# Attention in a four-layer kernel: maxima added by unit matrix products, values split by ScalarE and VectorE, by-key logits ahead of the weighing

## The chip, the cores and the metric

One core of a Trainium2 chip runs the whole program in one launch. The metric is the device time of one execution, in microseconds (us): the kernel before takes 1793.18 us, the median of three runs (1792.56 to 1794.38). The engines are PE (TensorE, matrix products; PEld its weight loads), DVE (VectorE), ACT (ScalarE), POOL (GpSimd) and SP (SyncE, which here issues nearly all DMAs). PSUM has 8 banks per partition; PE writes only there, POOL reads and writes only SBUF.

## The reference

Four layers on x of shape 16 x 14 x 14 x 192, each with a group norm before it and a residual sum behind it: a GRU over the 196 positions, attention (l1), a mixture of 8 experts with 2 chosen per token, attention again (l3). The change is in the attention, 16 images, 196 tokens, 12 heads of 16 channels:

```python
q, k, v = (qkv[0], qkv[1], qkv[2])
rel_h = jnp.einsum('bhwc,hkc->bhwk', qr, Rh)
rel_w = jnp.einsum('bhwc,wkc->bhwk', qr, Rw)
bias = rel_h[..., :, None] + rel_w[..., None, :]
attn = jnp.einsum('bqd,bkd->bqk', q * scale, k)
attn = attn + bias.reshape(B * nh, N, N)
attn = jax.nn.softmax(attn, axis=-1)
out = jnp.einsum('bqk,bkd->bqd', attn, v)
```

Results are held close to float32: an operand is split into a high part rounded to fp32r and a low part (the rest), and products are summed over the parts.

## The kernel before

`attention_layer` is called twice, for l1 and l3, with the same loop. It first makes q and k (`item`), v (`value`) and the position terms (`rel`), and stores q, k and `rel` to DRAM. Then comes the main loop: IMAGES = 96 steps, one step for one image and one pair of heads (6 pairs x 16 images), with LAG = 4. Each engine runs its own list of work in program order; semaphores are the only order between them.

For image g of the loop the work is:

- `logits_by_query(g)` (PE, L1159): four products, queries in partitions and keys in columns, into two banks that exist once. Only the maxima are taken from them.
- VectorE (L1388): the maximum of each query over the keys, 98x784 to 98x4, in PSUM; then a cast to bf16 (L1393) and the rest in bf16 (L1395), into `mt`.
- `maxima_to_rows(g)` (PE, L1168): four products with a diagonal of ones turn `mt` into two rows; ScalarE copies these (L1316) into rows 0 and 1 of q, against which k holds rows of -1. So the next product subtracts the maximum.
- `logits_by_key(g)` (PE, L1180): four products, keys in partitions and queries in columns, with the maximum subtracted, into one of two pairs of banks. It waits for L1316 and for the exponentials of g - 2.
- ScalarE: the exponential twice, rounded (`ph`, L1325) and in float32 (`p32`, L1328). POOL: `pl` = `p32` - `ph` (L1080), in a ring of 3.
- `weigh_values(g)` (PE, L1197 and L1198): eight products of v (high and low part, and a column of ones) with `ph` and `pl`, into one bank. VectorE copies out the 64 product rows (L1361) and the 2 rows of sums (L1364); the next weighing waits for both copies.

v is split into its two parts by POOL (`split_values`, L1047 and L1051), for four images at a time in two head parts, spread over the three steps that follow each fourth step. Every eighth step VectorE takes a reciprocal of the sums (L1368).

In 28 of the 96 steps (1 to 7, 11 to 17, 33 to 39, 43 to 49, `rel_of_step`) a `rel` item of the next four heads runs as well: six products on PE (L1144 to L1146), a rounding on ScalarE (L1290), a subtraction on VectorE (L1353). Its bank exists once, so PE's next `rel` waits for VectorE's subtraction. Items 1 to 7 of 14 and 8 to 14 are of two shapes, with a DRAM store of the tile between them.

The order of a step i is written out by hand. On PE: `logits_by_query(i)`, `maxima_to_rows(i - 1)`, `rel`, `weigh_values(i - 4)`, `logits_by_key(i - 1)`. On VectorE: the maximum of i with cast and rest, the two copies of i - 4, `rel`, the reciprocal. On ScalarE: the copy of the maxima of i - 1, the exponentials of i - 2, `rel`. SP loads q, k, `rel` and, as a fourth piece, two zero rows of q for a quarter of the next pair, spread over the steps.

Of the kernel before, what the change touches and what calls it, by code (L numbers as in the profile page):

```python
# [7 lines left out]
ALU = mybir.AluOpType  # L8
# [702 lines left out]
ROWS = 106  # L711
Q_ROWS, REL_ROWS = 2, 50
# [33 lines left out]
def attention_layer(nc, tag, ins, x_in, y_out, qk_dram, rel_dram, sums_dram, rec_dram, given=None, kept=None, extra=(), taken=None, ahead=None, x_here=None, x_stored=None):  # L746
# [8 lines left out]
    LOADS, SLOTS, LOWS = 4, 3, 3  # L755
    PARTS = 4
    EACH = B // PARTS
    with Scope(nc, tag) as s:
# [43 lines left out]
        mt, ones_at = s.sb("mt", [128, 4, 2], bf16), s.sb("ones_at", [128, TH], bf16)  # L802
# [18 lines left out]
        s_summed, mx_ready, mh_ready, ml_ready = (s.sem(n) for n in "s_summed mx_ready mh_ready ml_ready".split())  # L821
        x_ready, x_copied, t_summed, p_high, p_ready, pl_ready = (s.sem(n) for n in "x_ready x_copied t_summed p_high p_ready pl_ready".split())
# [23 lines left out]
        def rel_sums(r):  # L846
            return ps[:56, rel_bank(r), :448].rearrange("p (u b w) -> p u b w", u=2, b=B)

# [17 lines left out]
        with nc.Block() as block:  # L866
            @block.sync
            def _(sp):
# [43 lines left out]
                def load(p, part, piece):  # L912
# [14 lines left out]
                    dst, row, src = ((q, Q_ROWS, qk[0]), (k, Q_ROWS, qk[1]), (q, REL_ROWS, rel), (q, 0, k[ROWS:ROWS + 2]))[piece]  # L927
                    rows = 2 if piece == 3 else src.shape[0]
# [26 lines left out]
                def main_step(i):  # L955
                    p, b = divmod(i, B)
                    part, piece = divmod(b - EACH - 1, LOADS)
                    if i < IMAGES and p + 1 < PAIRS and part >= 0:
                        load(p + 1, part, piece)
                    if i < IMAGES and p > 0 and part < 0:  # L960
                        load(p, (b + B - EACH - 1) // LOADS, (b + B - EACH - 1) % LOADS)
# [49 lines left out]
            def _(pool):  # L1011
# [24 lines left out]
                def split_values(n):  # L1036
                    p, part = divmod(n, 4)
                    halves, slots = slice(8 * part, 8 * part + 8), slice(n % 2 * 8, n % 2 * 8 + 8)
                    def whole(head):
                        return v[:TH, halves, 32 * p + HD * head:32 * p + HD * head + HD]  # L1040

                    def place(head, low):
                        at = 32 * head + HD * low
                        return vs[:TH, slots, head, at:at + HD]

                    def high(head):
                        pool.tensor_copy(place(head, 0), whole(head)).then_inc(vh_ready, 1)  # L1047

                    def low(head):
                        pool.wait_ge(vh_ready, 2 * n + head + 1)  # L1050
                        pool.tensor_tensor(place(head, 1), whole(head), place(head, 0).bitcast(f32), ALU.subtract).then_inc(vl_ready, 1)  # L1051

                    return high, low

# [15 lines left out]
                for n in range(2):  # L1070
                    high, low = split_values(n)
                    for head in range(2):
                        high(head)
                    for head in range(2):
                        low(head)
                for g in range(IMAGES):
# [5 lines left out]
                    if 5 <= g < IMAGES - 4 and g % 4:  # L1082
                        n = (g + 3) // 4
                        high, low = split_values(n)
                        if g % 4 == 1:
                            pool.wait_ge(o_summed, 4 * n - 4)
                            high(0)
                        if g % 4 == 2:
                            high(1)
                            low(0)  # L1090
                        if g % 4 == 3:
                            low(1)
# [11 lines left out]
            def _(pe):  # L1104
# [44 lines left out]
                def logits_by_query(g):  # L1149
# [3 lines left out]
                    if g >= 1:  # L1153
                        pe.wait_ge(ml_ready, g)
# [8 lines left out]
                def maxima_to_rows(g):  # L1163
                    pe.wait_ge(ml_ready, g + 1)
                    if g >= 1:
                        pe.wait_ge(x_copied, g)
                    for n in range(4):
                        last = pe.matmul(ps[64:66, R_BANK, n * TH:n * TH + TH], mt[:TH, n, :], ones_at[:TH, :], start=True, stop=True)  # L1168
                    last.then_inc(x_ready, 1)

                def logits_by_key(g):
                    b = g % B
                    pe.wait_ge(x_copied, g + 1)
                    if g >= 2:
                        pe.wait_ge(p_ready, g - 1)
                    queries = slice(b * T, (b + 1) * T)
                    for head in range(2):
                        for half in range(2):
                            keys = slice(b * T + half * TH, b * T + (half + 1) * TH)
                            last = pe.matmul(ps[:TH, T_BANK + 2 * (g % 2) + head, half * T:half * T + T], k[:, head, keys],  # L1180
                                             q[:, head, queries], start=True, stop=True)
                    last.then_inc(t_summed, 1)
# [1248 lines left out]
```

## Time and profile before

| what | value |
|---|---|
| median of 3 timed runs | 1793.18 us |
| profiled execution, first to last instruction | 1796.6 us |
| first maximum of l1's main loop starts at | 642.8 us |
| last copy of the sums of l1's main loop starts at | 905.45 us |
| last maximum of l3's main loop starts at | 1737.1 us |
| PE, VectorE, ScalarE, POOL busy over the span | 83%, 71%, 54%, 48% |

The profile is of one execution. Its span is from the first to the last instruction; what lies around it is not in the profile. A row of time says when an instruction (or a merged row of several, "x4") started, how long it took, and in brackets how long its engine had been idle before it and what ended that. PE's matrix products overlap: their spacing, not their length, is what each costs.

### The profile page before, as it was taken

The page shows a single profiled execution, that of the slowest core. Times are in us where ns is not written, and L with a number is a line of the kernel's source. Part 1 is how long each engine was busy: PE and PEld are TensorE (multiplying, and loading weights), DVE is VectorE, ACT ScalarE, POOL GpSimd, SP SyncE. Part 2 cuts the span into 40 slices and gives each one's busy share as a digit, 9 for nine tenths or more (in the row PEclk, how much of TensorE's full clock was granted, in tenths as well). Part 3 has the DMA queues.
Part 4 walks back from the last instruction along what each step waited for, and adds up shares of the span by engine and source line. Part 5 has one row for each costly group of instructions (what it writes and reads, how often), then busy time and mean ns, then how long its engine had stood idle before and what let it go on. Part 6 is the DMA issues. An engine that isn't in the chain of part 4 may idle for free. (4 is left out here: it accounts for less than half of the span.)

```text
span 1796.6 us, 51708 instructions
## 1 busy us (share of the span) xinstructions
PE 1485.9 (83%) x19315; PEld 1272.1 (71%) x19315; DVE 1269.7 (71%) x4444; ACT 973.4 (54%) x1990; POOL 855.0 (48%) x1080
## 2 busy tenths in 40 slices
PE   4868888888876888889977999899998697888978
PEld 4757777777765776767755667678774586777766
DVE  7877787877778567879956684544446646888974
ACT  3633333333344567889924234555543556888972
POOL 2712222222235056879952111456551416787984
PEclk9955555555558889999986589899995798999998
DMA  3000000000002596667215204322225468666712
GB/s 87 1 20 4 4 5 4 4 4 4 4 3 83 171 257 151 147 156 161 58 48 173 98 24 151 125 81 86 83 73 153 144 159 254 166 147 150 146 29 58
DMA packets 72178, 165.21 MB, mean 92 GB/s; under 512 B 17938, under 2 KB 43162, under 8 KB 69436
## 3 DMA queue, kind: packets, MB, share of 16 engines
q1 hardware_dynamic: 66556, 149.05, 31.3%
q0 software_dynamic: 5376, 12.85, 2.3%
q8 instruction: 158, 2.59, 0.6%
q14 instruction: 88, 0.72, 0.1%
HBM read 93.84 MB, written 67.42 MB: 90 GB/s over the span
## 5 line engine op out<-in xcount | busy, mean ns | idle before, releaser
L1080 POOL TENSOR_TENSOR l_arena<-l_arena,l_arena 98x784 fp32r<-98x784 f32 x192 | 358.4, 1872 | 91.3 <-ACT l_arena L1328 79.0
L514 PE MATMUL gru_ps_r<-gru_hp,gru_wp 128*128 128x16 f16 x3920 | 200.1, 176 | 68.1 <-DVE gru_hp L489 68.1
L514 PEld LDWEIGHTS gru_ps_r<-gru_hp,gru_wp 128*128 128x128 f16 x3920 | 150.8, 106 | 88.5 <-DVE gru_hp L489 88.5
L567 POOL TENSOR_TENSOR gru_kept<-gru_keep,l0s_state 128x32 f32<-128x32 f32 x196 | 49.3, 251 | 305.4 <-ACT gru_keep L582 305.4
L1388 DVE TENSOR_REDUCE l_ps<-l_ps 98x4 f32<-98x784 f32 x192 | 187.5, 977 | 9.1 <-PE l_ps L1159 3.2
L514 PE MATMUL gru_ps_n<-gru_hp,gru_wp 128*128 128x16 f16 x3920 | 191.1, 174 | 0.0
L1197 PE MATMUL l_ps<-l_arena,l_arena 128*66 128x196 f32 x768 | 162.1, 264 | 20.9 <-POOL l_arena L1080 20.1
L580 ACT ACTIVATE gru_reset<-gru_ps_r,gru_unscale 128x32 f32<-128x32 f32 x196 | 56.4, 288 | 216.8 <-PE gru_ps_r L514 216.8
L1325 ACT ACTIVATE l_arena<-l_ps 98x784 fp32r<-98x784 f32 x192 | 158.4, 825 | 4.6
L1328 ACT ACTIVATE l_arena<-l_ps 98x784 f32<-98x784 f32 x192 | 157.0, 818 | 0.0
L1198 PE MATMUL l_ps<-l_arena,l_arena 128*66 128x196 f32 x768 | 155.0, 255 | 0.0
L514 PEld LDWEIGHTS gru_ps_n<-gru_hp,gru_wp 128*128 128x128 f16 x3920 | 150.0, 104 | 0.0
L1197 PEld LDWEIGHTS l_ps<-l_arena,l_arena 128*66 128x66 f32 x768 | 106.5, 139 | 41.0 <-POOL l_arena L1080 30.8
L1316 ACT ACTIVATE l_arena<-l_ps 2x392 fp32r<-2x392 f32 x192 | 94.1, 490 | 74.0 <-PE l_ps L1168 67.3
L1159 PE MATMUL l_ps<-l_arena,l_arena 128*98 128x196 f32 x768 | 110.7, 267 | 18.8 <-DVE l_mt L1395 13.7
L1159 PEld LDWEIGHTS l_ps<-l_arena,l_arena 128*98 128x98 f32 x768 | 85.6, 168 | 34.3 <-DVE l_mt L1395 25.3
L1198 PEld LDWEIGHTS l_ps<-l_arena,l_arena 128*66 128x66 f32 x768 | 107.0, 139 | 1.2
L1361 DVE COPY l_arena<-l_ps 64x196 f32<-64x196 f32 x192 | 67.7, 353 | 54.5 <-PE l_ps L1198 51.0
L1180 PE MATMUL l_ps<-l_arena,l_arena 128*98 128x196 f32 x768 | 103.5, 258 | 0.0
L1144 PE MATMUL l_ps<-l_arena,l_arena 128*56 128x224 f32 x168 | 59.8, 356 | 43.1 <-DVE l_arena L1353 40.4
L2231 DVE TENSOR_TENSOR l_arena<-mx_ps,l_arena 128x512 fp32r<-128x512 f32 x56 | 38.7, 692 | 77.9 <-ACT l_arena L2039 52.2
L1838 POOL DMA_INDIRECT picked<-l_arena,mx_target x56 | 55.3, 987 | 71.9 <-DVE l_arena L2238 60.5
(389 smaller groups left out, 4568.9 us busy)
## 6 DMA issues: line engine op xcount, KB each, us to landing
l_arena<-qk SPq DMA_DIRECT2D x96, 294.0 KB
qk<-l_arena SPq DMA_DIRECT2D x48, 392.0 KB, 9.0
rel<-l_arena SPq DMA_DIRECT2D x24, 686.0 KB
l_arena<-rel SPq DMA_DIRECT2D x48, 343.0 KB
qk<-l_arena SPq DMA_DIRECT2D x12, 784.0 KB, 7.9
l_arena<-in_experts_dram SPq DMA_DIRECT2D x8, 1152.0 KB, 7.6
l_arena<-x SPq DMA_DIRECT2D x24, 294.0 KB, 5.3
l_arena<-x SPq DMA_DIRECT2D x24, 196.0 KB, 3.1
```

The costliest lines, as they stand in the source:

```text
L514: last = pe.matmul(out[:, b, B * m:B * m + B], wp[:, wi, g, m, :], hp[:, b, part, B * k:B * k + B], start=False, stop=True, skip_group_che ...
L1080: pool.tensor_tensor(pl[g % LOWS][:TH, :, :], p32[:TH, g % 2, :, :], ph[:TH, g % 4, :, :].bitcast(f32), ALU.subtract).then_inc(pl_ready, 1)
L1144: pe.matmul(out, rh[:, n, :], line(high), start=True, stop=False)
L1159: last = pe.matmul(ps[:TH, S_BANK + head, half * T:half * T + T], q[:, head, queries], k[:, head, keys], start=True, stop=True)
L1180: last = pe.matmul(ps[:TH, T_BANK + 2 * (g % 2) + head, half * T:half * T + T], k[:, head, keys], q[:, head, queries], start=True, stop=True)
L1197: pe.matmul(out, values, ph[:, g % 4, head, cols], start=head == 0 and keys == 0, stop=False)
L1198: last = pe.matmul(out, values, pl[g % LOWS][:, head, cols], start=False, stop=head == 1 and keys == 1)
L1316: act.activation(q[0:2, :, b * T:(b + 1) * T], ps[64:66, R_BANK, :TB].rearrange("p (h t) -> p h t", h=2), ACT.Copy).then_inc(x_copied, 1)
L1325: act.activation(ph[:TH, g % 4, :, :], banks, ACT.Exp).then_inc(p_high, 1)
L1328: act.activation(p32[:TH, g % 2, :, :], banks, ACT.Exp).then_inc(p_ready, 1)
L1361: dve.tensor_copy(o_quad[p // 2][row:row + 64, b * T:(b + 1) * T], ps[:64, O_BANK, :T]).then_inc(o_kept, 1)
L1388: dve.tensor_reduce(m, ps[:TH, S_BANK:S_BANK + 2, :TB].rearrange("p c (h k) -> p c h k", h=2), AXIS.X, ALU.max).then_inc(mx_ready, 1)
```

## The change

- The maxima no longer go through rows of q. VectorE writes the negated maximum straight into `mt` (fp32r, in SBUF, a ring of 2). After the four by-key products, still in the same accumulation, PE adds four products: a column of `mt` broadcast to 98 columns as weights, and a unit matrix, read twice, as the moved operand of 196 columns. So each by-key logit gets the negative maximum of its query. `maxima_to_rows`, the cast, the rest and ScalarE's copy go; q and k lose two rows (ROWS 106 to 104), and SP's fourth load piece goes.
- On PE `logits_by_key(i - 1)` with the unit products now comes ahead of `weigh_values(i - 4)`, behind `rel`.
- v is split by ScalarE (`round_values`, behind the exponentials in two of four steps) and VectorE (`lower_values`, between the maximum and the copies in two of four steps), not by POOL. The first two parts are made ahead of the loop.

```diff
-    LOADS, SLOTS, LOWS = 4, 3, 3
+    LOADS, SLOTS, LOWS = 3, 3, 3
-        mt, ones_at = s.sb("mt", [128, 4, 2], bf16), s.sb("ones_at", [128, TH], bf16)
+        mt, unit = s.sb("mt", [128, 2, 4], f32r), s.sb("unit", [128, TH], f32r)
...
                 def logits_by_key(g):
                     b = g % B
-                    pe.wait_ge(x_copied, g + 1)
                     if g >= 2:
                         pe.wait_ge(p_ready, g - 1)
+                    both = unit[:TH, :].rearrange("p (a t) -> p a t", a=1).to_broadcast([TH, 2, TH])
                     for head in range(2):
+                        bank = ps[:TH, T_BANK + 2 * (g % 2) + head, :TB]
                         for half in range(2):
-                            last = pe.matmul(ps[:TH, T_BANK + 2 * (g % 2) + head, half * T:half * T + T], k[:, head, keys],
-                                             q[:, head, queries], start=True, stop=True)
+                            pe.matmul(bank[:, half * T:half * T + T], k[:, head, keys], q[:, head, queries],
+                                      start=half == 0, stop=False, skip_group_check=True)
+                    pe.wait_ge(max_ready, g + 1)
+                    for head in range(2):
+                        bank = ps[:TH, T_BANK + 2 * (g % 2) + head, :TB].rearrange("p (k t) -> p k t", k=2)
+                        for half in range(2):
+                            n = 2 * head + half
+                            last = pe.matmul(bank[:, :, half * TH:(half + 1) * TH], mt[:TH, g % 2, n:n + 1].to_broadcast([TH, TH]), both,
+                                             start=False, stop=half == 1, skip_group_check=True)
                     last.then_inc(t_summed, 1)
...
                     if i < IMAGES:
                         logits_by_query(i)
-                    if 1 <= i <= IMAGES:
-                        maxima_to_rows(i - 1)
                     if i in rel_of_step:
                         rel(rel_of_step[i])
+                    if 1 <= i <= IMAGES:
+                        logits_by_key(i - 1)
                     if i >= LAG:
                         weigh_values(i - LAG)
-                    if 1 <= i <= IMAGES:
-                        logits_by_key(i - 1)
...
+                def round_values(n, head):
+                    act.activation(value_parts(n, head, 0), values_of(n, head), ACT.Copy).then_inc(vh_ready, 1)
...
-                        act.activation(q[0:2, :, b * T:(b + 1) * T], ps[64:66, R_BANK, :TB].rearrange("p (h t) -> p h t", h=2), ACT.Copy).then_inc(x_copied, 1)
...
                         act.activation(p32[:TH, g % 2, :, :], banks, ACT.Exp).then_inc(p_ready, 1)
+                        n = g // 4 + 1
+                        if g >= 6 and n < IMAGES // 4 and g % 4 in (2, 3):
+                            act.wait_ge(o_summed, 4 * n - 4)
+                            round_values(n, g % 4 - 2)
...
+                def lower_values(n, head):
+                    dve.wait_ge(vh_ready, 2 * n + head + 1)
+                    dve.tensor_tensor(value_parts(n, head, 1), values_of(n, head), value_parts(n, head, 0).bitcast(f32), ALU.subtract).then_inc(vl_ready, 1)
...
                 for i in range(IMAGES + LAG):
                     if i < IMAGES:
                         dve.wait_ge(s_summed, i + 1)
-                        m = ps[:TH, S_BANK, 400:404]
-                        dve.tensor_reduce(m, ps[:TH, S_BANK:S_BANK + 2, :TB].rearrange("p c (h k) -> p c h k", h=2),
-                                          AXIS.X, ALU.max).then_inc(mx_ready, 1)
-                        dve.wait_ge(mx_ready, i + 1)
-                        if i >= 1:
-                            dve.wait_ge(x_ready, i)
-                        dve.tensor_copy(mt[:TH, :, 0], m).then_inc(mh_ready, 1)
-                        dve.wait_ge(mh_ready, i + 1)
-                        dve.tensor_tensor(mt[:TH, :, 1], m, mt[:TH, :, 0], ALU.subtract).then_inc(ml_ready, 1)
+                        if i >= 2:
+                            dve.wait_ge(t_summed, i - 1)
+                        dve.tensor_reduce(mt[:TH, i % 2, :], ps[:TH, S_BANK:S_BANK + 2, :TB].rearrange("p c (h k) -> p c h k", h=2),
+                                          AXIS.X, ALU.max, negate=True).then_inc(max_ready, 1)
+                    n = i // 4
+                    if 8 <= i < IMAGES and i % 4 in (2, 3):
+                        lower_values(n, i % 4 - 2)
                     if i >= LAG:
                         keep_products(i - LAG)
```

## Rows read from the trace of the kernel before

**Rows 1.** The page's first line.

```profile
span 1796.6 us, 51708 instructions
```

**Rows 2.** Windows of the maxima, L1388: stretch, its length, busy time, count, clock.

```profile
802.30:893.50 91.20, 40.29 (x41) 1.00 0.57 121
```

**Rows 3.** Windows, plain steps: PE, PEld, VectorE, ScalarE, POOL busy (count), clock, DMA.

```profile
802.30:893.50 91.20, 83.87 (x821) 69.91 (x820) 83.23 (x211) 83.19 (x124) 90.32 (x95) 1.00 0.57 121
```

**Rows 4.** Lines by group, same stretch: count, busy us, mean ns, idle before.

```profile
L1080 POOL TENSOR_TENSOR l_arena<-l_arena,l_arena 98x784 fp32r<-98x784 f32 x42 | 78.5, 1873 | 1.9 <-ACT l_arena L1328 1.5
...
L1368 DVE RECIPROCAL l_sums<-l_sums 98x32 f32<-98x32 f32 x5 | 1.6, 330 | 0.0
```

**Rows 5.** Timeline of VectorE in one plain step: start us, length us.

```profile
828.48 0.35 DVE L1361 COPY l_arena<-l_ps 64x196 f32<-64x196 f32 x1
...
829.26 0.98 DVE L1388 TENSOR_REDUCE l_ps<-l_ps 98x4 f32<-98x784 f32 x1
830.27 0.17 DVE L1393 CAST l_mt<-l_ps 98x4 bf16<-98x4 f32 x1
...
830.67 0.36 DVE L1361 COPY l_arena<-l_ps 64x196 f32<-64x196 f32 x1
```

**Rows 6.** Waits, 640 to 910 us: us in total, times, longest.

```profile
DVE l_arena L1361 <- PE l_ps L1198: 25.1, 34, 1.6
PEld l_ps L1144 <- DVE l_arena L1353: 21.9, 22, 3.4
```

**Rows 7.** Timeline of PE in a step with a `rel` item of the second shape.

```profile
783.98 0.39 PE L1144 MATMUL l_ps<-l_arena,l_arena 128*56 128x224 f32 x1 [0.78 <-DVE l_arena L1353]
...
785.22 0.28 PE L1197 MATMUL l_ps<-l_arena,l_arena 128*66 128x196 f32 x1
785.33 0.25 PE L1198 MATMUL l_ps<-l_arena,l_arena 128*66 128x196 f32 x1
...
785.97 0.53 PE L1180 MATMUL l_ps<-l_arena,l_arena 128*98 128x196 f32 x4
786.34 0.53 PE L1159 MATMUL l_ps<-l_arena,l_arena 128*98 128x196 f32 x4
...
787.91 0.39 PE L1144 MATMUL l_ps<-l_arena,l_arena 128*56 128x224 f32 x1 [0.78 <-DVE l_arena L1353]
```

**Rows 8.** Timeline of VectorE in the same step.

```profile
786.17 0.35 DVE L1361 COPY l_arena<-l_ps 64x196 f32<-64x196 f32 x1 [0.97 <-PE l_ps L1198]
...
786.94 0.92 DVE L1353 TENSOR_TENSOR l_arena<-l_ps,l_arena 56x448 fp32r<-56x448 f32 x1
```

**Rows 9.** Timeline of PE in a `rel` step of the first shape.

```profile
752.04 0.32 PE L1144 MATMUL l_ps<-l_arena,l_arena 128*56 128x224 f32 x1 [0.48 <-DVE l_arena L1353]
...
755.16 0.32 PE L1144 MATMUL l_ps<-l_arena,l_arena 128*56 128x224 f32 x1 [0.49 <-DVE l_arena L1353]
```

**Rows 10.** Timeline, other stages: the nearest sizes from SBUF to SBUF.

```profile
557.78 0.19 DVE L159 TENSOR_TENSOR l_arena<-l_arena 96x32 f32<-96x32 f32 x1
...
1059.96 0.53 ACT L2014 ACTIVATE l_arena<-l_arena 128x392 fp32r<-128x392 f32 x1 [0.62 <-DVE l_arena L2189]
```

**Rows 11.** Timeline of the experts layer: VectorE and POOL at once.

```profile
965.13 0.60 POOL L1515 TENSOR_TENSOR l_arena<-l_arena,l_arena 64x196 fp32r<-64x196 f32 x1 [0.28 <-ACT l_arena L1568]
965.19 0.77 DVE L1624 TENSOR_TENSOR l_arena<-l_arena,l_arena 128x196 fp32r<-128x196 f32 x1
```

**Rows 12.** Timeline ahead of l1: two POOL casts merged, and VectorE.

```profile
559.11 5.54 POOL L1019 CAST l_arena<-l_arena 128x3136 fp32r<-128x3136 f32 x2 [7.66 <-DMA l_arena<-in_attention_const_dram]
...
559.58 2.37 DVE L168 SCALAR_TENSOR_TENSOR l_arena<-l_arena 96x32 f32<-96x32 f32 x1
```

**Rows 13.** One line, L1624: least, median, greatest ns.

```profile
L1624 DVE TENSOR_TENSOR l_arena<-l_arena,l_arena x16: 346/350/772, 963.5 to 997.0; 128x196 fp32r<-128x196 f32 x16
```

**Rows 14.** Timeline of VectorE at the end of the loop of l1.

```profile
895.89 0.98 DVE L1388 TENSOR_REDUCE l_ps<-l_ps 98x4 f32<-98x784 f32 x1
...
905.45 0.36 DVE L1364 COPY l_arena<-l_ps 2x196 f32<-2x196 f32 x1
```

More of the change, by code:

```diff
@@ L710 @@
 QUADS = HEADS // 4
-ROWS = 106
-Q_ROWS, REL_ROWS = 2, 50
+ROWS = 104
+Q_ROWS, REL_ROWS = 0, 48
 AT_REL = 4 * N
@@ L847, in rel_sums, with values_of, value_parts @@
             return ps[:56, rel_bank(r), :448].rearrange("p (u b w) -> p u b w", u=2, b=B)
+        def values_of(n, head):
+            halves = slice(8 * (n % 4), 8 * (n % 4) + 8)
+            at = 2 * HD * (n // 4) + HD * head
+            return v[:TH, halves, at:at + HD]
+        def value_parts(n, head, low):
+            slots = slice(n % 2 * 8, n % 2 * 8 + 8)
+            at = 32 * head + HD * low
+            return vs[:TH, slots, head, at:at + HD]
         rel_of_step = {2 * B * quad + at: REL * (quad + 1) + j for quad in range(QUADS - 1) for j, at in enumerate(REL_STEPS)}
@@ L926, in load @@
                     rel = rel_dram[quad].rearrange("(g h r) c n -> g r c h n", g=2, h=2)[at].rearrange("r c h n -> (r c) h n")
-                    dst, row, src = ((q, Q_ROWS, qk[0]), (k, Q_ROWS, qk[1]), (q, REL_ROWS, rel), (q, 0, k[ROWS:ROWS + 2]))[piece]
-                    rows = 2 if piece == 3 else src.shape[0]
+                    dst, row, src = ((q, Q_ROWS, qk[0]), (k, Q_ROWS, qk[1]), (q, REL_ROWS, rel))[piece]
+                    rows = src.shape[0]
                     sp.dma_start(dst[row:row + rows, :, cols].bitcast(f32), src[:, :, cols].bitcast(f32)).then_inc(quarter_in[part], 16)
@@ L956, in main_step @@
                     p, b = divmod(i, B)
-                    part, piece = divmod(b - EACH - 1, LOADS)
-                    if i < IMAGES and p + 1 < PAIRS and part >= 0:
+                    part, piece = divmod(b - EACH - 1, EACH)
+                    if i < IMAGES and p + 1 < PAIRS and part >= 0 and piece < LOADS:
                         load(p + 1, part, piece)
-                    if i < IMAGES and p > 0 and part < 0:
-                        load(p, (b + B - EACH - 1) // LOADS, (b + B - EACH - 1) % LOADS)
+                    if i < IMAGES and p > 0 and part < 0 and piece < LOADS:
+                        load(p, part + PARTS, piece)
                     if i % 5 == 3 and i < 50:
@@ L1161, in logits_by_query @@
                     last.then_inc(s_summed, 1)
[L1163 to L1169, printed above, removed]
                 def logits_by_key(g):
                     b = g % B
-                    pe.wait_ge(x_copied, g + 1)
                     if g >= 2:
@@ L1299, in constants @@
                     act.wait_ge(const_in, 16)
-                    act.activation(ones_at[:TH, :], ident[:TH, :], ACT.Copy).then_inc(ident_ready, 1)
+                    act.activation(unit[:TH, :], ident[:TH, :], ACT.Copy).then_inc(ident_ready, 1)
                     act.wait_ge(pick_in, 16)
@@ L1383, in _ @@
                 last_order(item, lambda i: None)
+                def lower_values(n, head):
+                    dve.wait_ge(vh_ready, 2 * n + head + 1)
+                    dve.tensor_tensor(value_parts(n, head, 1), values_of(n, head), value_parts(n, head, 0).bitcast(f32), ALU.subtract).then_inc(vl_ready, 1)
+                for n in range(2):
+                    for head in range(2):
+                        lower_values(n, head)
                 for i in range(IMAGES + LAG):
```

45 lines of the change are left out of this document (7 added, 38 removed).

## The prediction

> **What bounds the kernel now.** I read the page first for the share of each part, then the counts of one line by stretch, then the waits, then single steps in order of time. The change lies in the 96-step main loop of the two attention layers, and both layers run it alike, so all is worked out for one layer and doubled. There are two kinds of step, with different limits.
>
> *Plain steps* (18 to 32 and 50 to 95, 61 per layer). One maximum (L1388) runs per step: 41 of them start in 91.2 us, so a step takes 2.22 us [rows 2]. In that stretch POOL is busy 90.3 of 91.2 us [rows 3], most of it with one subtraction a step, 1873 ns at L1080 [rows 4]. VectorE is no less tight: its five instructions of a step follow one another with gaps of about 0.03 us from 828.48 to 830.67, 2.19 us [rows 5]. PE and ScalarE have some 8 us of the 91 free [rows 3]. So two engines bound these steps at once, and relieving only one would bring nothing; the change relieves both.
>
> *Steps with a `rel` item* (1-7, 11-17, 33-39, 43-49). Here a loop through PE and VectorE binds. In the second kind (43-49): `rel` starts on PE at 783.98, the eight products of `weigh_values` follow at 785.22, VectorE copies their result out at 786.17, subtracts for `rel` at 786.94, and PE may start the next `rel` at 787.91 [rows 7, 8]: 1.24 + 0.95 + 0.77 + 0.97 = 3.93 us per step. PE runs `logits_by_key` at 785.97, behind the weighing, in time in which it waits for that loop anyway (idle 0.78 us ahead of 787.91). The first kind is the same loop with shorter items, 752.04 to 755.16, 3.12 us [rows 9]. The waits say so too: VectorE's copy waits for the weighing's last product 25.1 us, and PE's first `rel` weight waits for VectorE's subtraction 21.9 us, among the long ones of the loop [rows 6].
>
> **The change, part by part.**
>
> 1. *By-key logits ahead of the weighing.* In a `rel` step PE now runs `rel`, four by-key products, four unit products, then the weighing. All eight stand inside the loop above. The four by-key products take 0.37 us (785.97 to 786.34 [rows 7]). The unit products have the same 196 columns and type fp32r, and the accumulating products of the weighing advance at 0.09 us each (785.33 to 785.97 [rows 7]), so I take 0.37 us for these four as well. Below: they can hardly be under 0.37. Above: the `rel` products, which read 224 columns in wide strides, take 0.21 us each (783.98 to 785.22 for six [rows 7]), or 0.83 us for four. The moved 98 columns are contiguous, so I stay at 0.37. The loop grows by 0.74 us. Nothing hides it: `rel` waits for VectorE's `rel`, that stands behind the copies of the weighing, and these behind the weighing. Of the 28 steps, 1 to 3 have no weighing yet and 11 waits for the store of the earlier `rel` tile; 4-7, 12-17, 33-39 and 43-49 are 24. 24 x 0.74 = 17.8 us per layer, **+35.5 us**.
>
> 2. *VectorE in plain steps.* The cast and subtraction of the maximum go: from 830.27 to 830.67, 0.40 us [rows 5]. A step without value work is then 2.19 - 0.40 = 1.79 us on VectorE. In two of four steps `lower_values` is added, a subtraction of 98x128 with both inputs in SBUF. The trace has 96x32 in 0.19 us and 128x196 in 0.35 us, undisturbed [rows 10, 13], between them 0.28 us, with its gap 0.31: 2.10 us. A reciprocal of 0.33 us [rows 4] comes every eighth step as before.
>
> 3. *PE in plain steps.* Query, by-key and unit products are 3 x 0.37 = 1.11 us; from the weighing's start to the copy 0.95, the copies 0.77 [rows 7, 8], the maximum 0.98 and 0.05 until PE starts on it. The path query, weighing, copy, next maximum, query after that spans two steps: 1.11 + 0.95 + 0.77 + 1.03 = 3.86, or 1.93 us a step. Per four steps two at 2.10 and two at 1.93, 8.06 us; with a reciprocal in every second four, (8.06 + 8.42) / 8 = 2.06 us a step. Saved: 2.22 - 2.06 = 0.16 us, 61 steps, two layers, **-19.5 us**. Floor: VectorE alone, (2 x 1.79 + 2 x 2.10) / 4 + 0.33 / 8 = 1.99 us, or -28 us.
>
> 4. *Value splitting moved from POOL.* POOL loses 0.36 us a step (2.22 less 1.87) and has some 0.2 us free in each. But `lower_values` reads both inputs from SBUF while POOL's L1080 does the same, for 1.87 of about 2.1 us. The trace shows what happens then: VectorE's L1624, 0.35 us alone, took 0.77 us when it started 0.06 us into a POOL subtraction, and ended 0.23 us after POOL's 0.60 us were over [rows 11, 13]; a 96x32 operation took 2.37 us and ended at 561.95, just after the first of two POOL casts (559.11 plus half of 5.54 is 561.88) [rows 12]. So it waits until the running POOL instruction ends, then slips in ahead of the next. A subtraction that starts at a random point waits 0.88 x 1.87 / 2 = 0.82 us. Queued behind it on VectorE are the copies of the weighing, for which PE's next weighing waits, and the next maximum, for which the next query waits. Once one has waited, the next one of the pair starts 1.82 us after it (2.10 less its own 0.28), about when the POOL instruction that followed ends; so I count one wait a pair. The 61 plain steps hold 16 pairs: 16 x 0.82 x 2 layers = **+26.2 us**. Bounds: 0, and 52 us if both of a pair wait. In `rel` steps VectorE idles about 1 us ahead of the copy today [rows 8], and 0.40 + 0.74 more after the change, which covers the subtraction and most of its wait: 0.
>
> The Trainium skill, page "SBUF — State Buffer", section "Who interferes with whom", says the same in general: a VectorE instruction with two SBUF inputs and a GpSimd instruction that reads SBUF share one read interface, and whichever comes second blocks until the first is over. The rows agree (0.77 against 0.35 us). Without that rule part 4 would be 0 and the sum +11; with it, +37.
>
> 5. *ScalarE.* The copy of the maxima goes from each step; two roundings of 98x128 in four steps come (0.53 us at most, the row for 392 columns [rows 10]). ScalarE is on neither loop: 0. If its slack were gone it would delay POOL, which now has slack too.
>
> 6. *SP.* The fourth load piece, two rows copied inside SBUF, goes. No instruction of the loop waits for these loads: 0.
>
> 7. *Ends of the loop.* Ahead of the first maximum VectorE gets four subtractions, 4 x 0.31 = 1.2 us; steps 1 to 3 lose the maxima products and the ScalarE copy ahead of the exponentials, some 0.7 us each: net -0.9 us a layer, between -2 and +1.2. At the end, 9.6 us pass from the last maximum (895.89) to the last copy (905.45) [rows 14], since POOL is behind; with its backlog gone, between 0.5 and 2.4 us less, I take 1.5. Together **-4.8 us**.
>
> Sum: 35.5 - 19.5 + 26.2 - 4.8 = **+37.4 us**. The profiled execution spans 1796.6 us [rows 1], 3.4 us above the median 1793.2 of the timed runs; what changes lies inside the loops of both alike, so I add it to the median: **1831 us**, 2.1% slower.
>
> **The rivals.**
> - *No wait for SBUF.* VectorE's subtraction always falls into POOL's free 0.2 us. For it: the two engines run at one period and could lock so. Against: POOL runs nearly always. 35.5 - 19.5 - 4.8 = +11: **1804 us**.
> - *Every subtraction waits, or the unit products are dear.* Both of a pair: +63, 1857 us. Or 0.21 us per unit product: 0.46 us more in 24 x 2 `rel` steps is +22, with plain steps PE-bound about as today (+20 more): 1872 us. Against: the second of a pair finds POOL at its end. **1857 to 1872 us**.
> - *Faster: POOL was the only governor.* If the by-key and unit products in `rel` steps fell into time in which PE waits, these steps would stay at 3.12 and 3.93 us and the plain ones go to their floor of 1.99: 122 x 0.23 = 28, with the ends -33: **1760 us**. It decides if the copy in `rel` steps is late for another reason than the weighing; the trace shows VectorE idle 0.97 us until exactly the weighing's last product [rows 8], which speaks against it. A mixture (lengthened `rel` steps, floor elsewhere, no wait for SBUF, the larger gains at the ends of 3.6 us a layer) gives 35.5 - 28 - 7 = 0: no change, **1793 us**.
>
> **How the numbers follow.** The forecast has 0.55, no wait for SBUF 0.17, the dearer case 0.12, no change by the mixture 0.07, the faster one 0.09. From 1797 (the mixture with a little left) to 1862 (between the two dearer prices) is 0.8. A measurement can tell 0.2%, 3.6 us, from no change. Faster by more 0.09, within 0.07, slower 0.84.
>
> **What would show it.** Of the changed kernel: `rel` steps of 3.86 and 4.67 us between maxima, with the unit products between by-key and weighing; plain steps at 2.06 us on average where no subtraction waited; VectorE's subtraction of 98x128 at 0.28 us in some instances and well above 1 us in others, ending with POOL's; POOL busy under 95% of a plain stretch. `rel` steps no longer than now would refute part 1, subtractions all near 0.28 us part 4, and a plain step above 2.3 us without such waits part 3.

## The result, and the profile after

The changed kernel takes 1832.58 us, the median of four runs (1822.62 to 1835.51); the kernel before took 1792.87 us, the median of four (1789.83 to 1794.38). The ratio is 1.0215, with a 95% interval of 1.0188 to 1.0242: slower by 40 us. The forecast was 1831 us. The time came out within 2 us of it although several of the terms did not; the rows below show which.

The page's first line of the changed kernel, to set beside [rows 1]:

```profile
span 1833.3 us, 50706 instructions
```

Where the 36.8 us between the two spans lie can be read from the starts of the maxima, one per step (L1388 before, L1375 after). The table has the sum of the intervals from one maximum to the next, in us, for l1 / l3 (95 intervals a layer, 60 of them plain); "outside" is the span less the two loops. "h" and "w" are the `rel` steps of the first and the second shape.

| steps | before | after | difference, both layers |
|---|---|---|---|
| 0 to 3 | 13.0 / 12.5 | 9.1 / 9.1 | -7.4 |
| h: 4 to 7, 33 to 39 | 34.9 / 35.7 | 41.9 / 41.9 | +13.2 |
| w: 12 to 17, 43 to 49 | 53.1 / 52.9 | 69.4 / 70.8 | +34.1 |
| 8 to 11, 40 to 42 | 19.0 / 18.9 | 21.5 / 19.8 | +3.4 |
| plain: 18 to 32, 50 to 94 | 133.0 / 133.0 | 134.1 / 134.7 | +2.7 |
| both loops | 506.2 | 552.2 | +46.0 |
| outside | 1290.4 | 1281.1 | -9.3 |

**Plain steps.** Windows of the changed kernel over l1's plain steps, first the maxima alone (stretch, its length, busy time and count), then PE, PEld, VectorE, ScalarE and POOL, with clock and DMA last:

```profile
826.00:917.00 91.00, 40.64 (x42) 1.00 0.54 117
...
826.00:917.00 91.00, 84.23 (x832) 77.69 (x831) 83.84 (x150) 68.58 (x104) 80.27 (x52) 1.00 0.54 117
```

POOL is relieved: 80.3 of 91.0 us, where [rows 3] had 90.3 of 91.2. VectorE runs 150 instructions in place of 211 and is as busy as before. The groups by line in the same stretch, with count, busy time and mean ns, answer to [rows 4] and name the reason:

```profile
L1065 POOL TENSOR_TENSOR l_arena<-l_arena,l_arena 98x784 fp32r<-98x784 f32 x42 | 78.8, 1878 | 11.4 <-ACT l_arena L1303 9.4 <-PE l_ps L1172 0.4
L1365 DVE TENSOR_TENSOR l_arena<-l_arena,l_arena 98x128 fp32r<-98x128 f32 x21 | 15.9, 759 | 0.0
```

and of that one line the least, median and greatest ns:

```profile
L1365 DVE TENSOR_TENSOR l_arena<-l_arena,l_arena x21: 282/986/1315, 828.4 to 916.5; 98x128 fp32r<-98x128 f32 x21
```

An instruction of 0.28 us takes 0.76 us on average. Over the 64 of the plain steps of both layers the first of a pair takes 1.21 us on average and the second 0.32. VectorE and POOL at the end of l1's loop (start, length), to set beside [rows 5]:

```profile
915.58 0.97 DVE L1375 TENSOR_REDUCE l_mt<-l_ps 98x4 fp32r<-98x784 f32 x1
916.47 1.26 DVE L1365 TENSOR_TENSOR l_arena<-l_arena,l_arena 98x128 fp32r<-98x128 f32 x1
917.76 0.36 DVE L1340 COPY l_arena<-l_ps 64x196 f32<-64x196 f32 x1
...
919.42 0.28 DVE L1365 TENSOR_TENSOR l_arena<-l_arena,l_arena 98x128 fp32r<-98x128 f32 x1
```

```profile
913.79 5.76 POOL L1065 TENSOR_TENSOR l_arena<-l_arena,l_arena 98x784 fp32r<-98x784 f32 x3 [0.68 <-ACT l_arena L1303]
```

Three subtractions of POOL stand in one row, so the second ends at about 913.79 + 3.84 = 917.63 us; VectorE's first subtraction ends at 917.73. The second of the pair starts 2.95 us later, near the end of POOL's third (919.55), and waits for nothing. That is the pattern that part 4 of the prediction drew.

**Steps with a `rel` item.** PE in l1, first shape, the by-key products of three steps (compare [rows 9]), and the unit products behind the first:

```profile
753.72 0.53 PE L1147 MATMUL l_ps<-l_arena,l_arena 128*98 128x196 f32 x4
754.09 0.54 PE L1154 MATMUL l_ps<-l_unit,l_mt 98*98 98x196 f32 x4
...
757.60 0.52 PE L1147 MATMUL l_ps<-l_arena,l_arena 128*98 128x196 f32 x4
...
761.45 0.53 PE L1147 MATMUL l_ps<-l_arena,l_arena 128*98 128x196 f32 x4
```

3.88 and 3.85 us a step; the prediction had 3.86. Of the second shape, PE in two steps that follow one another (compare [rows 7]):

```profile
786.94 0.39 PE L1118 MATMUL l_ps<-l_arena,l_arena 128*56 128x224 f32 x1 [1.93 <-DVE l_arena L1332]
...
788.18 0.64 PE L1147 MATMUL l_ps<-l_arena,l_arena 128*98 128x196 f32 x4
788.61 0.87 PE L1154 MATMUL l_ps<-l_unit,l_mt 98*98 98x196 f32 x4
789.27 0.37 PE L1171 MATMUL l_ps<-l_arena,l_arena 128*66 128x196 f32 x1
...
790.58 0.87 PE L1133 MATMUL l_ps<-l_arena,l_arena 128*98 128x196 f32 x4
792.57 0.39 PE L1118 MATMUL l_ps<-l_arena,l_arena 128*56 128x224 f32 x1 [1.12 <-DVE l_arena L1332]
...
793.81 0.54 PE L1147 MATMUL l_ps<-l_arena,l_arena 128*98 128x196 f32 x4
794.19 0.54 PE L1154 MATMUL l_ps<-l_unit,l_mt 98*98 98x196 f32 x4
794.56 0.26 PE L1171 MATMUL l_ps<-l_arena,l_arena 128*66 128x196 f32 x1
...
795.29 0.53 PE L1133 MATMUL l_ps<-l_arena,l_arena 128*98 128x196 f32 x4
797.24 0.39 PE L1118 MATMUL l_ps<-l_arena,l_arena 128*56 128x224 f32 x1 [1.42 <-DVE l_arena L1332]
```

The second step, 792.57 to 797.24, is the predicted 4.67 us. The first is 5.63 us long. From by-key to query it takes 2.40 us where the second takes 1.48. Windows inside those two stretches, then one over both steps, and last one over steps 43 to 49 of l1 in the kernel before (the clock is the third number from the end):

```profile
788.60:790.50 1.90, 1.90 (x14) 1.90 (x13) 0.00 (x0) 1.74 (x3) 0.62 (x1) 0.50 0.34 105
...
794.10:795.30 1.20, 1.20 (x16) 1.20 (x15) 0.00 (x0) 1.20 (x2) 0.00 (x0) 1.00 0.00 0
...
785.00:795.00 10.00, 6.96 (x46) 6.12 (x46) 4.89 (x8) 6.14 (x10) 3.70 (x2) 0.83 0.70 158
```

```profile
768.00:796.00 28.00, 22.93 (x194) 18.88 (x194) 19.94 (x43) 21.90 (x30) 17.85 (x18) 1.00 0.56 122
```

The granted clock is 0.50 (1.2 GHz) in the long step, 1.00 (2.4 GHz) in the short one; the records of 14 products fall into 1.90 us there and of 16 into 1.20 us here. Of the 26 w steps of both layers, the clock stayed at 1.00 in seven, which took 4.01 to 5.00 us each; it fell in the other 19, which took 5.20 to 6.11. In the seven steps 43 to 49 it was 1.00 throughout before the change. PE had been idle 1.93 us ahead of the long step's `rel` and 1.12 us ahead of the other; before the change it was 0.78 [rows 7]. So the second shape costs 34 us and not the 19 that the prediction's term had for it.

The waits from 640 to 920 us (in total, times, longest) that answer to [rows 6] show both loops longer:

```profile
DVE l_arena L1340 <- PE l_ps L1172: 52.8, 52, 3.2
...
PEld l_ps L1118 <- DVE l_arena L1332: 36.7, 24, 6.3
```

### The profile page after: what moved, and what is told of

The parts are those of the page before. It is cut to its first block and busy times, and to the rows that moved or that the text cites. A ratio compares the mean times of both kernels' runs of the same rounds, so it can differ in the third digit from the quotient of the medians.

```text
span 1833.3 us, 50706 instructions
## 1 busy us (share of the span) xinstructions
PE 1495.7 (82%) x19315; PEld 1319.9 (72%) x19315; DVE 1263.4 (69%) x4156; ACT 900.0 (49%) x1894; POOL 800.5 (44%) x888
## 5 line engine op out<-in xcount | busy, mean ns | idle before, releaser
L1375 DVE TENSOR_REDUCE l_mt<-l_ps 98x4 fp32r<-98x784 f32 x192 | 186.8, 973 | 7.2 <-PE l_ps L1133 1.4
L1171 PE MATMUL l_ps<-l_arena,l_arena 128*66 128x196 f32 x768 | 164.9, 266 | 26.0 <-DVE l_arena L1343 26.0
L1172 PE MATMUL l_ps<-l_arena,l_arena 128*66 128x196 f32 x768 | 163.0, 264 | 0.0
L1171 PEld LDWEIGHTS l_ps<-l_arena,l_arena 128*66 128x66 f32 x768 | 112.2, 146 | 32.0 <-issue 23.6
L1133 PE MATMUL l_ps<-l_arena,l_arena 128*98 128x196 f32 x768 | 114.6, 273 | 18.1 <-DVE l_mt L1375 11.7
L1262 ACT ACTIVATE l_arena<-l_ps 56x448 fp32r<-56x448 f32 x84 | 62.6, 746 | 127.7 <-PE l_ps L1120 108.9
L1118 PE MATMUL l_ps<-l_arena,l_arena 128*56 128x224 f32 x168 | 58.3, 347 | 69.4 <-DVE l_arena L1332 66.8
L1172 PEld LDWEIGHTS l_ps<-l_arena,l_arena 128*66 128x66 f32 x768 | 112.0, 146 | 0.0
L1154 PE MATMUL l_ps<-l_unit,l_mt 98*98 98x196 f32 x768 | 107.8, 265 | 0.0
L1147 PE MATMUL l_ps<-l_arena,l_arena 128*98 128x196 f32 x768 | 105.4, 261 | 0.0
```

Of the source, the lines that this page charges most:

```text
L1118: pe.matmul(out, rh[:, n, :], line(high), start=True, stop=False)
L1133: last = pe.matmul(ps[:TH, S_BANK + head, half * T:half * T + T], q[:, head, queries], k[:, head, keys], start=True, stop=True)
L1147: pe.matmul(bank[:, half * T:half * T + T], k[:, head, keys], q[:, head, queries], start=half == 0, stop=False, skip_group_check=True)
L1154: last = pe.matmul(bank[:, :, half * TH:(half + 1) * TH], mt[:TH, g % 2, n:n + 1].to_broadcast([TH, TH]), both, start=False, stop=half == ...
L1171: pe.matmul(out, values, ph[:, g % 4, head, cols], start=head == 0 and keys == 0, stop=False)
L1172: last = pe.matmul(out, values, pl[g % LOWS][:, head, cols], start=False, stop=head == 1 and keys == 1)
```

## The experiments

All were timed together with the kernel before, 1 to 4 on one chip and 5 to 8 on another; the changed kernel stands here with its time from above. Of every one the table gives the median, the ratio to before with its interval, and from its profile the loop of one layer (mean of the two, us) split as above.

| kernel | us | ratio | 0-3 | h | w | 8-11, 40-42 | plain | loop | outside |
|---|---|---|---|---|---|---|---|---|---|
| before | 1793.0, 1790.8 | 1 | 12.8 | 35.3 | 53.0 | 19.0 | 133.0 | 253.1 | 1290.4 |
| changed | 1832.6 | 1.0188 to 1.0242 | 9.1 | 41.9 | 70.1 | 20.7 | 134.4 | 276.1 | 1281.1 |
| 1 weighing first | 1782.4 | 0.9912 to 0.9975 | 9.6 | 35.3 | 54.9 | 20.7 | 127.6 | 248.1 | 1285.4 |
| 2 one input in PSUM | 1805.2 | 1.0042 to 1.0102 | 9.6 | 41.9 | 71.0 | 19.3 | 120.3 | 262.0 | 1277.3 |
| 3 more products | 1820.5 | 1.0110 to 1.0225 | 10.1 | 41.8 | 62.0 | 18.6 | 134.8 | 267.3 | 1279.1 |
| 4 no unit products | 1804.4 | 1.0049 to 1.0102 | 9.9 | 37.9 | 63.0 | 20.0 | 126.7 | 257.5 | 1284.1 |
| 5 first in `rel` steps | 1795.9 | 1.0003 to 1.0045 | 9.1 | 35.5 | 52.8 | 22.5 | 133.5 | 253.2 | 1287.3 |
| 6 lowered on POOL | 1764.1 | 0.9830 to 0.9887 | 10.1 | 34.1 | 54.3 | 21.6 | 123.5 | 243.6 | 1277.6 |
| 7 by way of PSUM | 1777.3 | 0.9908 to 0.9952 | 9.3 | 35.3 | 54.6 | 21.3 | 124.8 | 245.3 | 1277.5 |
| 8 by PSUM, key first | 1772.4 | 0.9864 to 0.9916 | 9.1 | 35.0 | 52.7 | 23.3 | 121.7 | 241.8 | 1284.8 |

**1. Weighing first.** One part of the change undone:

```diff
-                    if 1 <= i <= IMAGES:
-                        logits_by_key(i - 1)
                     if i >= LAG:
                         weigh_values(i - LAG)
+                    if 1 <= i <= IMAGES:
+                        logits_by_key(i - 1)
```

> The changed kernel with one part undone: on PE the weighing of step i - 4 is again ahead of the by-key and unit products. Theory (the eight products stand inside the loop of PE and VectorE in the steps with a rel item, and the waiting that they add lets the granted TensorE clock fall in the second shape): the steps of the first shape go back from 41.9 to about 35 us per layer, those of the second shape from 70 to about 53, the granted clock is 1.00 there, the plain steps keep their mean of 2.24 us; 1832.6 - 2 x 24 = about 1785 us. Rival (the order does not matter, the unit products themselves or VectorE's subtraction lengthen the loop): only half or none of it comes back, 1815 us or more.

1782.4 us. h and w fell to 35.3 and 54.9 us, so the order is what lengthened these steps; the rival is out. Behind the weighing the unit products cost nothing in the h steps (35.3 us before too); in the w steps 1.9 us a layer are left. But two things of the expectation missed. The clock over the w steps of l1 was 0.94, not 1.00:

```profile
766.00:795.00 29.00, 23.78 (x186) 20.71 (x184) 20.89 (x31) 18.00 (x26) 14.51 (x10) 0.94 0.56 122
```

And the plain steps gained too, 127.6 us in place of 134.4. So the expected 1785 us came near in part by luck: in the profiles h and w gave back 43.5 of the 48 us counted on, and the plain steps 13.5 that were not. In them the subtraction waits far less (least, median, greatest ns, against 282/986/1315):

```profile
L1365 DVE TENSOR_TENSOR l_arena<-l_arena,l_arena x21: 282/351/530, 807.2 to 888.8; 98x128 fp32r<-98x128 f32 x21
```

**2. One input in PSUM.** The wait for POOL taken away by other data:

```diff
-                def lower_values(n, head):
+                def lower_values(n, head, psum=False):
...
+                    taken_off = ps[:TH, R_BANK, :8 * HD].rearrange("p (a c) -> p a c", a=8) if psum else value_parts(n, head, 0).bitcast(f32)
-                    dve.tensor_tensor(value_parts(n, head, 1), values_of(n, head), value_parts(n, head, 0).bitcast(f32), ALU.subtract).then_inc(vl_ready, 1)
+                    dve.tensor_tensor(value_parts(n, head, 1), values_of(n, head), taken_off, ALU.subtract).then_inc(vl_ready, 1)
...
-                        lower_values(n, i % 4 - 2)
+                        lower_values(n, i % 4 - 2, psum=18 <= i < 33 or i >= 50)
```

> The changed kernel, but in the plain steps VectorE's subtraction of the value parts takes its second input from a PSUM bank that is idle there, in place of SBUF: the same instruction on the same 98x128 elements with one input in SBUF (the low parts of v are then not the right ones). Theory (a VectorE instruction with two SBUF inputs waits for POOL's running one): the subtraction takes about 0.28 us in every instance, the plain steps fall from 2.24 to about 2.06 us, 61 x 0.18 x 2 = 22 us less, about 1811 us. Rival (the subtraction is slow for its access pattern or the path through PE binds these steps anyway): plain steps stay above 2.2 us and the time at 1830 to 1835 us.

1805.2 us. The subtraction and the engines in l1's plain steps from 826 us on (least, median, greatest ns; then the window as above):

```profile
L1366 DVE TENSOR_TENSOR l_arena<-l_arena,l_ps x19: 276/278/280, 831.7 to 903.3; 98x128 fp32r<-98x128 f32 x19
...
831.00:903.00 72.00, 71.00 (x720) 66.83 (x717) 65.32 (x131) 58.72 (x91) 69.06 (x47) 1.00 0.57 120
```

No instance waits, and the plain steps fall to 120.3 us, 2.00 us each, with h and w unchanged. So the wait is worth 134.4 - 120.3 = 14.1 us per layer, 28 in both, against 26.2 predicted. The same instruction with the same elements beside the same POOL work differs only in where one input lies. The Trainium skill, page "SBUF — State Buffer", section "Who interferes with whom", has a VectorE instruction with at most one SBUF input, outside its two-port modes, not contend with GpSimd; the trace agrees, 0.28 us in all 19.

**3. More products.** PE's waiting filled in the w steps:

```diff
+                def idle_products(i, count):
+                    keys = slice(i % B * T, (i % B + 1) * T)
+                    pe.wait_ge(p_ready, i - 2)
+                    for n in range(count):
+                        pe.matmul(ps[:TH, T_BANK + 2 * ((i - 1) % 2), :T], q[:, n % 2, keys][:, :TH], k[:, n % 2, keys], start=True, stop=True)
...
                     if i in rel_of_step:
+                        if 12 <= i < 18 or 43 <= i < 50:
+                            idle_products(i, 8)
                         rel(rel_of_step[i])
```

> The changed kernel with eight extra products of 196 columns a step on PE ahead of the rel item, in the 13 steps of the second shape only; they write banks that the by-key logits overwrite, nobody reads them, and they run in time in which PE waits (1.4 us ahead of the rel item). Theory (the long ones of these steps are long because the clock fell to 1.2 GHz after PE had waited): the granted clock stays at 1.00, all 13 steps take about 4.7 us, 61 us per layer in place of 70, about 1813 us. Rival 1 (another cause, such as VectorE's subtraction or a load): no change, 1832 us. Rival 2 (no time is free there): 13 x 0.72 = 9 us more per layer, 1851 us.

1820.5 us. By the time alone this is unclear (the interval reaches 1833); the profile is not. A window over its w steps 43 to 49, and PE in them:

```profile
776.00:808.00 32.00, 27.86 (x242) 24.81 (x241) 18.62 (x32) 17.17 (x26) 13.18 (x10) 1.00 0.49 107
```

```profile
785.12 0.39 PE L1118 MATMUL l_ps<-l_arena,l_arena 128*56 128x224 f32 x1 [0.69 <-DVE l_arena L1340]
...
788.21 0.90 PE L1141 MATMUL l_ps<-l_arena,l_arena 128*98 128x196 f32 x8
789.79 0.39 PE L1118 MATMUL l_ps<-l_arena,l_arena 128*56 128x224 f32 x1 [0.68 <-DVE l_arena L1340]
```

The clock stays at 1.00, and of the 13 steps all but the first and last of each stretch take 4.66 to 4.69 us in both layers; w falls from 70.1 to 62.0 us although PE has eight products more in each step. That leaves 62.0 - 53.0 = 9.0 us per layer for what the order itself costs, close to 13 x 0.74 = 9.6, and puts 8.1 us per layer on the clock. The Trainium skill, page "TensorE: Matmul & The Clock Gate", Part 1, lets the clock follow how busy the engine has been of late; this run agrees, for the only thing added is work.

**4. No unit products.**

```diff
-                            pe.matmul(bank[:, half * T:half * T + T], k[:, head, keys], q[:, head, queries],
-                                      start=half == 0, stop=False, skip_group_check=True)
+                            last = pe.matmul(bank[:, half * T:half * T + T], k[:, head, keys], q[:, head, queries], start=True, stop=True)
...
-                    for head in range(2):
-                        bank = ps[:TH, T_BANK + 2 * (g % 2) + head, :TB].rearrange("p (k t) -> p k t", k=2)
-                        for half in range(2):
-                            n = 2 * head + half
-                            last = pe.matmul(bank[:, :, half * TH:(half + 1) * TH], mt[:TH, g % 2, n:n + 1].to_broadcast([TH, TH]), both,
-                                             start=False, stop=half == 1, skip_group_check=True)
```

> The changed kernel without the four unit products (the maximum is not subtracted from the logits, the rest is as it was, the wait for the maximum too). Theory (they cost 0.37 us a step inside the loop of the rel steps): the first shape goes from 3.85 to 3.48 us a step, 41.9 to about 38 us per layer; the second shape loses 0.37 us a step or more, if the clock falls less often; the plain steps, where every second pair waits for POOL, lose up to 0.09 us. 2 x 24 x 0.37 = 18 and up to 11 us: 1803 to 1815 us. Rival (dear, 0.83 us for four): 2 x 24 x 0.83 = 40 us less, below 1793 us. Rival (cheap, hidden): 1832 us.

1804.4 us, in the range of the theory. The first shape loses 4.0 us in 11 steps, 0.36 each; two `rel` starts in l1 show the expected 3.48 us:

```profile
743.35 0.32 PE L1118 MATMUL l_ps<-l_arena,l_arena 128*56 128x224 f32 x1 [1.12 <-DVE l_arena L1325]
...
746.83 0.32 PE L1118 MATMUL l_ps<-l_arena,l_arena 128*56 128x224 f32 x1 [1.12 <-DVE l_arena L1325]
```

So a unit product costs 0.09 us; broadcast weights and an operand read twice make none dearer. The second shape still has long steps (63.0 us), and the plain steps lose 7.7 us per layer, 0.13 each, somewhat more than expected.

**5. Weighing first in the `rel` steps only.**

```diff
+                    first = i in rel_of_step
+                    if first and i >= LAG:
+                        weigh_values(i - LAG)
                     if 1 <= i <= IMAGES:
                         logits_by_key(i - 1)
-                    if i >= LAG:
+                    if not first and i >= LAG:
                         weigh_values(i - LAG)
```

> The changed kernel with the weighing ahead of the by-key and unit products again, but only in the steps with a rel item; in the plain steps by-key and unit products stay ahead. With the weighing first everywhere the plain steps had fallen to 2.13 us, which I had not expected. Theory (in the plain steps the eight products ahead of the weighing leave VectorE no slack, so each time that its subtraction waits for POOL, the next maximum is late; with the weighing first the copies are ready in time and the wait costs less): rel steps as with the weighing first, 35 and 55 us per layer, plain steps again at 2.24 us: 1782 + 13 = about 1795 us. Rival (the plain steps gained because of how they begin after shorter rel steps, not by their own order): plain steps 2.13 us, 1782 us.

1795.9 us. The plain steps are back at 133.5 us while h and w are those of the kernel before. So the gain of experiment 1 in the plain steps comes from their own order.

**6. The subtraction on POOL,** with the weighing first everywhere:

```diff
+                    n = g // 4 + 1
+                    if g >= 6 and n < IMAGES // 4 and g % 4 in (2, 3):
+                        head = g % 4 - 2
+                        pool.wait_ge(vh_ready, 2 * n + head + 1)
+                        pool.tensor_tensor(value_parts(n, head, 1), values_of(n, head), value_parts(n, head, 0).bitcast(f32), ALU.subtract).then_inc(vl_ready, 1)
...
```

> Weighing first in all steps, and the subtraction of the value parts on POOL in place of VectorE, behind pl in two of four steps; ScalarE rounds as in the change. Theory (VectorE is free of the wait, and POOL becomes the bound of the plain steps: 1.87 us, 0.18 us a step for half of the earlier split, gaps of 0.05): plain steps about 2.10 us, rel steps as with the weighing first: 1776 to 1782 us. Rival (POOL no bound in these steps): 1.99 us, about 1766 us.

1764.1 us, below the theory's range and near the rival's value. The profile decides for the theory, with the time set too high. All engines in l1's plain steps:

```profile
800.00:885.00 85.00, 80.73 (x819) 75.95 (x818) 69.70 (x129) 67.12 (x104) 84.50 (x72) 1.00 0.64 128
```

POOL is busy 84.5 of 85 us and binds them at 2.06 us (2.10 expected, 1.99 by the rival). The loops are 4.5 us a layer shorter than in experiment 1; the rest of the 18 us between the medians lies outside them as far as the profiles show it (1277.6 against 1285.4 us).

**7 and 8. The values by way of PSUM.** Experiment 2 with the right values: in the plain steps ScalarE also copies the unrounded values to the idle bank. 7 has the weighing first everywhere, 8 in the `rel` steps only.

```diff
...
                 def round_values(n, head):
+                    if in_psum(n):
+                        act.wait_ge(vl_ready, 2 * n)
+                        act.activation(psum_values(head), values_of(n, head), ACT.Copy)
                     act.activation(value_parts(n, head, 0), values_of(n, head), ACT.Copy).then_inc(vh_ready, 1)
...
-                    dve.wait_ge(vh_ready, 2 * n + head + 1)
-                    dve.tensor_tensor(value_parts(n, head, 1), values_of(n, head), value_parts(n, head, 0).bitcast(f32), ALU.subtract).then_inc(vl_ready, 1)
+                    dve.wait_ge(vh_ready, 2 * n + (2 if in_psum(n) else head + 1))
+                    whole = psum_values(head) if in_psum(n) else values_of(n, head)
+                    dve.tensor_tensor(value_parts(n, head, 1), whole, value_parts(n, head, 0).bitcast(f32), ALU.subtract).then_inc(vl_ready, 1)
```

> Weighing first in all steps, and in the plain steps ScalarE also copies the unrounded values to the idle PSUM bank, from which VectorE takes its first input, so that its subtraction has one input in SBUF. Theory (no wait for POOL is left, VectorE is the bound with 1.79 us, two of four times 0.31 and a reciprocal in eight): plain steps 1.99 us, rel steps as with the weighing first: 1782 - 14 = about 1768 us. Rival (with the weighing first the wait is already hidden, 0.38 us a subtraction, and something else holds 2.13 us): about 1782 us.

> The same values by way of PSUM, with the weighing first in the steps with a rel item only. Theory (without the wait for POOL, VectorE binds the plain steps in either order): plain steps 2.0 us as in the run with one input in PSUM, about 1769 us. Rival (the path query, by-key, unit, weighing, copy, maximum binds at 1.93 to 2.1 us): plain steps 2.06 us or more, 1777 us or more.

1777.3 and 1772.4 us. With the wait gone, the order with by-key first is the better one in plain steps (121.7 against 124.8 us), the reverse of experiments 1 and 5; 7 came out between its two theories, with 2.08 us a step in place of 1.99 or 2.13; what holds it was not found. 8 takes 2.03 us a step, between its theory (2.0) and its rival (2.06 or more) and nearer the theory; but its reason, that VectorE binds, is not shown. VectorE is busy 78.8 of 87 us in l1's plain steps, PE 85.5:

```profile
795.00:882.00 87.00, 85.50 (x865) 80.66 (x866) 78.82 (x158) 74.85 (x131) 83.37 (x56) 1.00 0.64 135
```

The versions 1, 6, 7 and 8 beat both the kernel before (by 0.6 to 1.4%) and the changed one. 6 and 8 are the fastest; their intervals overlap, and 8 has the shorter loops (241.8 against 243.6 us a layer), 6 the shorter rest, so which of them is better stays open.

## Why the prediction was right

**Part 1, by-key and unit products inside the loop of the `rel` steps: right in mechanism and in its price per step, too small in the second shape.** The step of 3.86 us was measured at 3.85 to 3.88; each of the four by-key and four unit products costs what was taken (0.37 us from the by-key row at 753.72 to the unit row at 754.09, and experiment 4). In the second shape the term was 13 x 0.74 x 2 = 19 us and came to 34. The missing 15 us are the clock: the prediction took the durations of [rows 7], all at a granted clock of 1.00, for a loop in which PE would wait longer. It noted that PE waits 0.78 us there and did not ask what the engine does in a longer wait. With the wait filled, 16 us came back in both layers and 9.0 a layer stayed, against the 9.6 predicted (experiment 3).

**Parts 2 and 3, plain steps without the wait: right, and somewhat too cautious.** 2.06 us was predicted, 2.00 measured in experiment 2, close to the floor of 1.99 that VectorE sets alone. Whether VectorE holds these steps there is not shown: PE is busy 71.0 of the 72.0 us, VectorE 65.3. Gain: (133.0 - 120.3) x 2 = 25 us, not 19.5.

**Part 4, the wait for SBUF: right.** One wait in each pair, ending with POOL's instruction; 28 us against 26.2. The starts are not random, as the price assumed: most first ones of a pair wait between 0.7 and 1.0 us. With parts 2 and 3 the plain steps come to +2.7 us in place of +6.7. What the prediction did not see is that this price depends on PE's order: with the weighing first, the same subtraction waits 0.07 us in the median (experiment 1). Why the two engines then fall in step was not tried.

**Parts 5 and 6.** POOL fell from 99% to 88% of the plain stretch, as forecast, and no row names ScalarE or SP as a new limit.

**Part 7, the ends.** The first four steps gave 7.4 us; the prediction had 3 x 0.7 a layer for them, 4.2. The four subtractions ahead of them, priced at 1.2 us a layer, do not show in l1, whose first maximum starts at 642.5 us (642.8 before). Windows over the first steps, before and after, hold one reason that the prediction had not: PE ran at a lower clock there before the change (0.66 of full speed, then 1.00). The third is experiment 3, which runs these steps as the changed kernel does:

```profile
642.00:652.00 10.00, 7.37 (x48) 6.25 (x48) 4.69 (x11) 4.27 (x7) 6.38 (x12) 0.66 1.04 222
```

```profile
642.00:652.00 10.00, 7.30 (x65) 6.59 (x66) 6.68 (x11) 6.65 (x10) 7.04 (x6) 1.00 1.04 232
```

```profile
642.80:652.90 10.10, 8.67 (x58) 8.44 (x58) 5.75 (x8) 6.41 (x10) 5.82 (x6) 0.66 1.04 238
```

There the clock was 0.66 and the four steps took 10.1 us, against 9.1 at 1.00. So the clock is worth about 1 us a layer of the 3.7, and it is not shown that the change is what raised it.

The gain at the other end did not come. From the last maximum to the last copy it is 9.63 us, to set beside the 9.56 of [rows 14]:

```profile
918.53 0.97 DVE L1375 TENSOR_REDUCE l_mt<-l_ps 98x4 fp32r<-98x784 f32 x1
...
928.16 0.36 DVE L1343 COPY l_arena<-l_ps 2x196 f32<-2x196 f32 x1
```

**The sum.** The two loops grew by 46 us. Of the forecast's 37.4 us, 38.0 lie between the first maximum and the last: the 1.2 us a layer ahead of the first and the 1.5 behind the last lie outside. The 8 us more are 15 in the w steps, less 4 in the plain steps, 3 in the h steps and 3 in the first four, and 3 more in steps 8 to 11 and 40 to 42, which were not priced. Step 11 waits for the store of the `rel` tile and was 1.7 us longer in l1; in steps 10 and 42 the subtraction waited as well. Outside the loops, where all these kernels run nearly the same code, the profiled execution before took 9.3 us longer. Over the ten profiles of the table that remainder lies between 1277.3 and 1290.4 us, and the one of before is the longest; so most of these 9 us can't be put down to the change. The 40 us between the medians are thus 6 less than the loops of the two profiled executions differ by. So it is luck that the total came within 2 us: the w steps were priced 15 us too low, and that was made up for by the plain, h and first four steps, which came out 10 us cheaper than priced, and by those 6 us. Whether the w steps of other executions have fewer long ones stays open.

## What to carry to other kernels

Where engines meet in a loop, cost an instruction by where it stands in the loop: in the `rel` steps eight products of 0.09 us were free behind the weighing and cost 0.74 us a step ahead of it. When a change lengthens PE's waiting, ask what clock the products after the wait will get, and price the step at both levels. Before moving a two-input VectorE instruction beside a busy POOL, look for an input that can lie in PSUM, or leave the instruction on POOL: both were faster here (8 against 5, and 6 against 1).

## What the hardware showed that I had not expected

- The six `rel` products of the second shape advance at 0.21 us each at either clock: they take 1.24 us from 786.94 to 788.18 at a granted clock of 1.00 and 1.28 us in step 12, from 681.81 to 683.09, at 0.50. The products behind them do follow the clock (1.48 against 2.40 us). Why these six do not was not tested. Step 12, the window first:

```profile
681.80:683.00 1.20, 1.19 (x6) 1.14 (x7) 0.96 (x1) 0.56 (x2) 0.76 (x1) 0.50 0.01 3
...
681.81 0.43 PE L1118 MATMUL l_ps<-l_arena,l_arena 128*56 128x224 f32 x1 [6.17 <-DVE l_arena L1332]
...
683.09 0.84 PE L1147 MATMUL l_ps<-l_arena,l_arena 128*98 128x196 f32 x4
```

- The clock fell inside a running loop: from 785 to 795 us PE worked 6.96 of 10 us and was idle for 1.93 us at most at a time. Eight products of 0.09 us in each such step kept it up.
- The same two-input subtraction waits 0.7 us in the median or 0.07 us (l1's second plain stretch), depending only on the order of PE's work.
